# Keeping the three bfloat16 parts of the normed rows as bfloat16 in the convolution stage of a one-core kernel

## What is computed

```python
def binarize(w, H=1.0):
    return jnp.where(w >= 0, H, -H)

def _ln_c(v, eps=1e-06):                       # over the 64 channels
    m, s = jnp.mean(v, -1, keepdims=True), jnp.var(v, -1, keepdims=True)
    return (v - m) / jnp.sqrt(s + eps)         # _ln_t: the same with eps 1e-05

x = x + conv_general_dilated(_ln_c(x), binarize(kernel), strides (1, 1), 'SAME')   # 3 x 3, 64 -> 64
t = to_tokens(x)
t = t + graph_gated_experts(_ln_t(t), ..., edge_index)
```

## Time and profile before

| | us |
|---|---|
| Median of 3 runs | 2055.55 |
| Lowest and highest | 2052.54, 2056.61 |
| Profiled execution, its own time | 2052.51 |
| Its span | 2050.7 |
| Busy in the span: DVE, POOL, PE, ACT | 1410.4, 1010.9, 938.9, 478.6 |
| Mean granted clock of PE, of 1 | 0.613 |
| Busy from 720 to 908 us: DVE, PE, ACT | 152.3, 89.5, 63.8 |

### The profile page before, as it was taken

How to read it: one execution, slowest core, us unless ns; L and a number is a source line. 1 busy time by engine, 2 the same in 40 slices (tenths; PEclk the granted TensorE clock), 3 DMA queues, 4 the chain that set the end, 5 groups by cost and what they waited for, 6 DMA issues and landing times. The chain is left out here.

```text
span 2050.7 us, 38311 instructions
## 1 busy us (share of the span) xinstructions
PE 938.9 (46%) x13313; PEld 731.9 (36%) x13313; DVE 1410.4 (69%) x2954; ACT 478.6 (23%) x957; POOL 1010.9 (49%) x889
## 2 busy tenths in 40 slices
PE   1223222488888435548963443444434444344200
PEld 1222212366666335532223333343333343334200
DVE  6998999889988488861134655666556665566698
ACT  1222311254554224324431111111111111111110
POOL 0244554466665300000017777777777777777100
PEclk9995555576666557769985555555555555555555
DMA  6000000111111510101000011000000000010000
GB/s 134 10 22 17 24 23 22 39 42 40 42 39 40 126 4 0 41 10 12 0 2 11 11 11 12 10 11 10 12 10 11 10 11 11 11 12 10 4 21 20
DMA packets 113591, 46.59 MB, mean 23 GB/s; under 512 B 92503, under 2 KB 108591, under 8 KB 112802
## 3 DMA queue, kind: packets, MB, share of 16 engines
q0 software_dynamic: 27712, 20.51, 5.6%
q1 hardware_dynamic: 83666, 21.85, 5.6%
q10 hardware_dynamic: 2064, 2.10, 0.5%
HBM read 28.98 MB, written 15.89 MB: 22 GB/s over the span
## 5 line engine op out<-in xcount | busy, mean ns | idle before, releaser
L283 POOL DMA_INDIRECT edges_rows<-table,edges_src x576 | 653.7, 1135 | 178.8 <-issue 175.2
L183 DVE TENSOR_TENSOR sorting_keys<-sorting_keys 128x1024 f32<-128x1024 f32 (+1 forms) x392 | 372.0, 989 | 20.7 <-ACT sorting_keys L264 18.8
L675 POOL DMA_INDIRECT y_rows<-mixture_yt,mixture_xin x143 | 182.8, 1278 | 130.6 <-ACT mixture_yt L890 84.3
L670 POOL DMA_INDIRECT x_rows<-mixture_sent,mixture_slot x128 | 158.8, 1241 | 155.9 <-DVE mixture_slot L732 117.4
L1815 ACT ACTIVATE edges_hotT<-edges_hot_ps 128x1024 bf16<-128x1024 bf16 x74 | 71.7, 1021 | 665.0 <-PE edges_hot_ps L1848 665.0
L1753 DVE TENSOR_TENSOR edges_raw<-edges_rows,edges_side 128x64 f32<-128x64 f32 x36 | 8.0, 221 | 282.6 <-DMA edges_rows<-table,edges_src 282.6
L994 PE MATMUL mixture_bank<-mixture_xT,sorting_w_part 128*128 128x128 bf16 x858 | 118.7, 262 | 48.1 <-DVE mixture_hidden L817 28.6
L1886 PE MATMUL edges_score_bank<-all_ident,edges_score 128*64 128x128 f32 x36 | 14.1, 393 | 261.1 <-DVE edges_score L1755 261.1
L1643 POOL IOTA edges_part_i<- 128x64 int32 x1 | 0.2, 181 | 238.6 <-SPq L1534 238.6
L994 PEld LDWEIGHTS mixture_bank<-mixture_xT,sorting_w_part 128*128 x858 | 86.0, 107 | 83.6 <-issue 74.9
L1342 PE MATMUL convolve_turned<-all_ident,convolve_parts 128*128 128x128 f32 x256 | 51.1, 383 | 113.8 <-DVE convolve_parts L398 113.8
(11 more groups left out here) (379 smaller groups left out, 2557.9 us busy)
## 6 DMA issues: line engine op xcount, KB each, us to landing
edges_rows<-table,edges_src POOLq DMA_INDIRECT x576, 2.4
mixture_xin<-x_rows SPq DMA_DIRECT2D x143, 49.0 KB, 1.8
all_eo<-y_rows SPq DMA_DIRECT2D x16, 256.0 KB, 4.0
y_rows<-mixture_yt,mixture_xin POOLq DMA_INDIRECT x143
sorting_w<-in_L_ffn_w_dram SPq DMA_DIRECT2D x4, 512.0 KB, 8.8
x_rows<-mixture_sent,mixture_slot POOLq DMA_INDIRECT x128, 2.3
out_dram<-all_x_sb SPq DMA_DIRECT2D x8, 256.0 KB
constants_src_i<-in_L_ffn_edge_index_dram SPq DMA_DIRECT2D x1, 1024.0 KB, 4.8
```

The lines of the kernel that those rows point to most:

```text
L183: self.st.mark(dve.tensor_tensor(target[half], source[0], source[1], (ALU.min, ALU.max)[half]))
L283: pool.indirect_dma_start(to, None, rows, where).then_inc(done, 16)
L670: pool.indirect_dma_start(x_rows, bass.IndirectOffsetOnAxis(ap=slot[g % 2][:, c, t:t + 1], axis=0), now[c][:, t, :], None).then_inc(scatte ...
L675: pool.indirect_dma_start(y_rows, bass.IndirectOffsetOnAxis(ap=xin[j % XB][:, ROWX - 2:ROWX - 1].bitcast(U32), axis=0), yt[j % YB][:, :], ...
```

## The change

`split_rows` no longer has `rough`: it rounds the row straight into its slot of `parts`, which is now bfloat16, and subtracts that slot. The three copies and two subtractions stay, and the two widening casts go. `parts` and `parts4` become bfloat16, and PE turns them against `ident16`, a bfloat16 copy of the identity that DVE makes once at the start of the stage (so `signed` counts to 6). The two tiles `turned` are read and written as bfloat16 and take half the PSUM: the eight turned tiles of a half lie in 2 KB of a partition and not in 4 KB. ACT's reads have a bfloat16 source. No instruction changes its place in an engine's order.

```diff
-def split_rows(dve, st, y, rough, parts, ready):
+def split_rows(dve, st, y, parts, ready):
 
     for n in (1, 0):
-        st.link(dve.tensor_copy(rough[:, :, :], y[:, :, :]))
-        st.mark(dve.tensor_copy(parts[:, :, n, :], rough[:, :, :]))
-        st.link(dve.tensor_tensor(y[:, :, :], y[:, :, :], rough[:, :, :], ALU.subtract))
+        st.link(dve.tensor_copy(parts[:, :, n, :], y[:, :, :]))
+        st.link(dve.tensor_tensor(y[:, :, :], y[:, :, :], parts[:, :, n, :], ALU.subtract))
     dve.tensor_copy(parts[:, :, 2, :], y[:, :, :]).then_inc(ready, 1)
...
-        parts = a.sb("parts", [P, TB, 3, C])
+        parts = a.sb("parts", [P, TB, 3, C], BF16)
         y4 = a.sb("y4", [P, TB, C])
-        parts4 = a.sb("parts4", [P, TB, 3, C])
-        rough = a.sb("rough", [P, TB, C], BF16)
+        parts4 = a.sb("parts4", [P, TB, 3, C], BF16)
+        ident16 = a.sb("ident16", [P, P], BF16)
...
-        turned = [a.ps(f"turned{n}", [P, TB * P]) for n in range(2)]
+        turned = [a.ps(f"turned{n}", [P, TB * P // 2]) for n in range(2)]
...
             st.mark(dve.memset(signs[0:C, 1, :], 0.0))
+            st.mark(dve.tensor_copy(ident16[:, :], ident[:, :]))
             st.link(dve.memset(padded[:, :, :, :, :], 0.0))
...
-                    image = turned[n][:, :].rearrange("c (r w) -> c r w", w=S)
+                    image = turned[n][:, :].bitcast(BF16).rearrange("c (r w) -> c r w", w=S)
...
-                    act.activation(stacks[n][:, bass.ds(b * TB * P, TB * P)], turned[n][:, :], ACT.Copy)\
+                    act.activation(stacks[n][:, bass.ds(b * TB * P, TB * P)], turned[n][:, :].bitcast(BF16), ACT.Copy)\
...
-                        ins = pe.transpose(turned[n][:, t * P:(t + 1) * P], stacked, ident[:, :])
+                        ins = pe.transpose(turned[n][:, :].bitcast(BF16)[:, t * P:(t + 1) * P], stacked, ident16[:, :])
```

More of the change, by code:

```diff
@@ L1248, in _ @@
             st.mark(dve.memset(signs[0:C, 1, :], 0.0))
+            st.mark(dve.tensor_copy(ident16[:, :], ident[:, :]))
             st.link(dve.memset(padded[:, :, :, :, :], 0.0))
-            spare = dve.alloc_register(f"dve_spare_{a.phase}"), signed, 5
+            spare = dve.alloc_register(f"dve_spare_{a.phase}"), signed, 6
             def before(b):
-                st = LoopSteps(dve, steps2, b, 12)
+                st = LoopSteps(dve, steps2, b, 10)
                 n2.vector(dve, st, y[:, :, :], x_sb[:, bass.ds(b * TB, TB), :], b, normed2)
-                split_rows(dve, st, y, rough, parts, y_ready)
+                split_rows(dve, st, y, parts, y_ready)
                 st.end()
             def behind(b):
-                st = LoopSteps(dve, steps3, b, 13)
+                st = LoopSteps(dve, steps3, b, 11)
                 xb = x_sb[:, bass.ds(b * TB, TB), :]
@@ L1264, in behind @@
                 dve.wait_ge(y4_turned, 2 * b + 2)
-                split_rows(dve, st, y4, rough, parts4, y4_ready)
+                split_rows(dve, st, y4, parts4, y4_ready)
                 st.end()
@@ L1298, in _ @@
         def _(act):
-            act.wait_ge(signed, 5)
+            act.wait_ge(signed, 6)
             def pad(b, first):
@@ L1330, in _ @@
         def _(pe):
-            pe.wait_ge(signed, 5)
-            spare = pe.alloc_register(f"pe_spare_{a.phase}"), signed, 5
+            pe.wait_ge(signed, 6)
+            spare = pe.alloc_register(f"pe_spare_{a.phase}"), signed, 6
             def turn(source, ready, b, free, free_at, done):
```

## The result

The changed kernel takes 2037.37 us (median of 4 runs, 2035.07 to 2040.64) against 2055.93 us for the kernel before (4 runs). The ratio is 0.9914, 95% interval [0.9897, 0.9932]: 0.86% faster, 18.6 us between the medians. The forecast was 2035.4 us in a range of 2031 to 2044.

The account below looks back on a forecast made before the run. DVE was taken to set the pace in the convolution stage, with PE's transposes on its path. Gains of 10.9 + 9.3 - 0.5 + 0.75 - 0.25 = 20.2 us from the 2055.55 median gave 2035.4 us, range 2031 to 2044.

Parts of the forecast that it names:

- (1): Splits on DVE: removing 32 widening casts at 0.34 us each gains 10.9 us; spread bfloat16 slots cost nothing extra.
- Rival D: DVE's copies into bfloat16 slots take 0.69 us and not 0.43, giving 2047.4 us; chance 9%.
- (2): DVE's wait for ACT's square root: shorter bfloat16 transposes free ACT's queue sooner, gaining 9.3 us (bounds 8 and 9.5).
- Rival E: ACT's padded copies become slow and set the pace; at twice a whole read each, 2064 us; chance 3%.
- (3): Inside the loop, DVE sometimes waits for PE's convolution, depending on when the clock rises: -0.5 us (bounds 0 and 1.7).
- (4): Behind the loop, where DVE waits for PE from first transpose to convolution end: 0.75 us gained (bounds 0.2 and 1.3).
- (5): One more DVE operation, the 128 by 128 identity copy: -0.25 us.
- (6): ACT's reads of bfloat16 instead of float32 banks take as long as now: nothing gained or lost.
- rival B: Bfloat16 transposes do not help PE's clock up, so convolutions end later: 2038.8 us; chance 12%.
- the time behind the stage: Sign: the part of the run after 907 us should last as long as now, within 2 us.
- Rival C: PE's clock does not rise in time at all because its bursts become shorter: 2050.8 us; chance 4%.
- the case near D: The transposes save nothing in this stage and only the removed casts count: 2044.9 us; chance 2%.

Follow-up runs that it names:

- filler: The changed kernel with extra bfloat16 matmuls on PE, which nobody reads, issued while PE would be idle: 2036.06 us, ratio 0.9897 to the kernel before.

## Where the prediction was right and where not

The forecast of 2035.4 us was 2 us under the median. The mechanism was right: the two gains came as priced. What was mis-sized is what PE takes back. By its own steps, in the stage, where the sum can be checked to tenths:

- **(1) The casts, 10.9 us: right.** The stage's first split took 3.39 us from its first copy to DVE's next operation (730.43 to 733.82) and takes 2.72 (730.34 to 733.06), 16 x 0.67 = 10.7. The rounding into spread bfloat16 slots takes the same 0.43 us, and the subtraction that reads them 0.69 as before (a timeline of the changed kernel's DVE):

```profile
763.79 0.43 DVE L395 CAST convolve_parts<-convolve_y 128x512 bf16<-128x512 f32 x1
764.25 0.69 DVE L396 TENSOR_TENSOR convolve_y<-convolve_y,convolve_parts 128x512 f32<-128x512 f32 x1
764.97 0.43 DVE L395 CAST convolve_parts<-convolve_y 128x512 bf16<-128x512 f32 x1
```

Rival D falls with these rows. Taking the gap between starts (0.34 us) and not the cast's own 0.427 was the choice that mattered; the longer figure would have given 13.7.

- **(2) The root wait, 9.3 us: right**, 9.4. Counting ACT's queue forward from `parts4` ready gave the end of the second read and the variance at the same moment, 3.40 us; in the image above the variance is ready 779.14 - 775.77 = 3.37 after it and the root starts at 3.40. The two met with nothing to spare; a slower read would have kept DVE waiting. Rival E falls as well: three padded copies take 2.81 us, where they took 2.80.

- **(3) The convolution, -0.5 us: mis-sized.** The waits inside the loop grew from 7 x 0.15 to 2.6 us, so 1.5 us were lost. **(4) Behind the loop, +0.75 us: wrong in sign.** From PE's first transpose to DVE's add it was 7.67 us and is 7.96:

```profile
858.71 1.86 PE L1342 MATMUL convolve_turned<-convolve_ident,convolve_parts 128*128 128x128 bf16 x16 [7.45 <-DVE convolve_parts L397]
...
860.37 6.19 PE L1351 MATMUL convolve_conv<-convolve_signs,convolve_padded 128*128 128x64 bf16 x144
866.67 0.69 DVE L1262 TENSOR_TENSOR all_x_sb<-all_x_sb,convolve_conv 128x512 f32<-128x512 f32 x1 [8.29 <-PE convolve_conv L1351]
```

Both have the same two causes. The first is the place where the clock rises. Three windows of 6 us from a burst's first transpose in the changed kernel, the latest, the earliest and the last of the seven with a turn in front, then the last one of the second trace of the kernel before and of the changed kernel beside it:

```profile
759.49:765.49 6.00, 6.00 (x99) 6.00 (x100) 5.38 (x12) 2.15 (x3) 0.00 (x0) 0.51 0.00 0
776.11:782.11 6.00, 6.00 (x145) 6.00 (x146) 5.38 (x12) 2.11 (x3) 0.00 (x0) 0.76 0.00 0
...
858.71:864.71 6.00, 6.00 (x103) 6.00 (x104) 0.00 (x0) 1.94 (x2) 0.00 (x0) 0.53 0.01 3
```

```profile
875.36:881.36 6.00, 6.00 (x116) 5.99 (x117) 0.00 (x0) 2.05 (x2) 0.00 (x0) 0.77 0.01 3
```

```profile
856.92:862.92 6.00, 6.00 (x104) 6.00 (x105) 0.00 (x0) 1.94 (x2) 0.00 (x0) 0.53 0.01 3
```

The first three give 5.9, 2.9 and 5.6 us, and the seven have a mean of 4.6; the seven of the kernel before had 4.0. That is not shown to be the shorter burst's doing: in the second trace of the kernel before the seven have a mean of 4.5, and in the two other traces of the changed kernel 4.3 and 4.4. Within one trace of the changed kernel bursts of the same work rise anywhere from 2.6 to 6.0 us after their start. I had taken one trace's mean as if it belonged to the burst. What does repeat is the last burst, which term (4) is about: 2.9 and 2.8 us in the two traces of the kernel before, 5.6, about 6.0 and 5.6 in the three of the changed kernel. There I had put 4.1. Why the rise comes where it does in a burst stays open.

The second cause is the step at the high clock, which was too short: 0.0267 us for a matmul, from 75 in 2.00 us. That count of a window includes the matmuls that reach into it from the left. The convolution of 144 at the high clock takes 4.36 us with the last one's 0.19, so the step is (4.36 - 0.19) / 144 = 0.029 us, 0.3 us more for a whole convolution. The Trainium skill has a formula for the gap of single matmuls (TensorE: Matmul & The Clock Gate, Back-to-back issue gap): columns divided by 2.4 GHz plus 2.5 ns, by which it is 29.2 ns for 64 columns. It adds that in a stream with a weight load before every matmul, as here, the formula counts too little at few columns. These rows do not bear that out: they give 29 ns. With 5.6 us for the rise and 0.029 for the step, the reckoning of step (3) puts the end of the last convolution 8.2 us after `parts4` ready (2.05 + 4.18 + 0.45 x 3.9 + 0.2); DVE waited 8.29. By the same reckoning, of the 1.0 us that (4) missed the later rise is some 0.7 and the step some 0.25.

- **(5) The identity copy, -0.25 us**: 0.23 us long, and the head of the stage is 0.25 us longer. **(6)** nothing, as said.

Sum of the measured terms: 10.7 + 9.4 - 1.5 - 0.3 - 0.25 = 18.05 us, against 18.0 in the stage. The forecast sum was 20.2; the 2.1 us between them are terms (3) and (4).

Two of the prediction's signs misled. L1262 waited for PE inside the loop by 1.08, 0.41 and 0.46 us, and more than 0.3 was to speak for rival B; but the transposes do bring the clock up, as the run with four times as many shows, so the sign could not tell B from a late rise. The other is the time behind the stage, above. Rival C, the clock never rising in time, did not come near: the clock rose in every burst. The run with the casts put back excludes the case near D, that only the casts count: it still gains 9.2 us in the stage.

## What to carry to other kernels

When an engine waits for a tiny operation of another, look at what stands ahead of that operation in the other's queue and who feeds it; here PE's transposes were on DVE's path with ACT's queue between them, and shortening them was worth as much as the casts taken from DVE itself. Price a removed operation that nobody waits for by the distance between starts, not by its length. And when a change moves the bound to PE, do not carry over the moment at which its clock rises from one trace: here it lay anywhere from 2.6 to 6.0 us into bursts of the same work, so price the latest rise as well as the mean. Count the step at the high clock from one whole group of matmuls and not from a window.

## What was not expected of the hardware

Bfloat16 transposes alone bring PE's granted clock from 0.5 to 1.0, 4.6 and 5.6 us after their start in the two bursts shown. A convolution of 144 matmuls that follows a turn at the low clock took between 4.95 and 6.29 us in the changed kernel's first trace, by when the clock rose, and 4.36 behind filler. One chip ran the edge loop in 1255 us where others take 873 to 880, with the same kernel and nearly the same time in the convolution stage (188.6 us against 189.4).
